# Residual before key variance, short power before the long one, and the choice of experts cut in two, in a two-layer adaLN kernel

## What is computed

```python
h = _layernorm(x) * (1 + ca) + sa
q = x @ w_q;  kv = x @ w_kv                  # 16 heads of 64, keys are values
q = q*cos + rot(q)*sin;  kv = kv*cos + rot(kv)*sin
lkv = _ln(concat([prev_window, window]), ln_local_g, ln_local_b)
pkv = softmax(gkv_seg @ w_proj)              # over the 16 tokens of a segment
gkv = _ln(einsum('bnsd,bnsr->bnrd', gkv_seg, pkv), ln_global_g, ln_global_b)
attn = softmax(masked(concat([q @ gkv.T, q @ lkv.T])))
x = x + ga * (attn @ concat([gkv, lkv]) @ w_out + b_out)
h = _layernorm(x) * (1 + cb) + sb            # input of the experts
topk_vals, topk_idx = top_k(h @ router_w, 2) # of 4 experts
```

## Time and profile before

| what | value |
|---|---|
| median of 3 runs | 1746.96 us (1745.7 to 1750.88) |
| the profiled execution | 1739.43 us |
| its span in the trace | 1737.6 us |
| PE, DVE, ACT, POOL busy over the span | 78%, 64%, 54%, 47% |
| layer-0 attention, slots 0 to 8 (97 to 661 us): PE, DVE, ACT, POOL busy | 441.9, 413.5, 341.0, 283.1 of 564 us |
| mean granted clock of TensorE there | 0.88 |

### The profile page before, as it was taken

How to read it: one execution, slowest core, us unless ns; L and a number is a source line. 1 busy time by engine, 2 the same in 40 slices (tenths; PEclk the granted TensorE clock), 3 DMA queues, 4 the chain that set the end, 5 groups by cost and what they waited for, 6 DMA issues and landing times. The chain is left out here.

```text
span 1737.6 us, 31729 instructions
## 1 busy us (share of the span) xinstructions
PE 1351.8 (78%) x8970; PEld 1077.2 (62%) x8970; DVE 1112.3 (64%) x2581; ACT 939.1 (54%) x2747; POOL 812.6 (47%) x824
## 2 busy tenths in 40 slices
PE   2267786697877984897998998994899988999552
PEld 0044564464645764897998897992566666676452
DVE  4575787877978544648447547442578888888522
ACT  1155564565756763666666666662556555555110
POOL 2446646555475312564665564663344544432103
PEclk7588898888988986999999999996889899989576
DMA  6300000000000005020020000006111111220063
GB/s 211 106 2 3 1 9 3 7 9 0 8 2 7 9 7 205 20 109 10 10 103 15 11 12 8 13 9 193 35 22 31 26 24 34 33 31 10 12 194 112
DMA packets 127182, 72.28 MB, mean 42 GB/s; under 512 B 78296, under 2 KB 118488, under 8 KB 126680
## 3 DMA queue, kind: packets, MB, share of 16 engines
q1 hardware_dynamic: 116664, 60.95, 12.3%
q0 software_dynamic: 3200, 6.56, 1.5%
q10 hardware_dynamic: 7200, 3.41, 0.7%
HBM read 53.26 MB, written 17.12 MB: 41 GB/s over the span
## 5 line engine op out<-in xcount | busy, mean ns | idle before, releaser
L1433 POOL TENSOR_TENSOR hl<-hid,hh 128x256 fp32r<-128x256 f32 x396 | 293.2, 742 | 221.2 <-ACT hh L1410 217.4
L1476 DVE SCALAR_TENSOR_TENSOR hid<-GU,gub,sg 128x256 f32<-128x256 f32 x396 | 190.3, 481 | 194.5 <-ACT sg L1404 111.8
L1304 PE MATMUL GU<-xh,wh 128*128 128x256 f32 x792 | 233.5, 295 | 39.4 <-DVE wl L1452 30.3
L1404 ACT ACTIVATE sg<-GU,gub 128x256 f32<-128x256 f32 x396 | 188.2, 475 | 123.6 <-PE GU L1306 122.1
L1305 PE MATMUL GU<-xl,wh 128*128 128x256 f32 x792 | 225.6, 285 | 0.0
L1306 PE MATMUL GU<-xh,wl 128*128 128x256 f32 x792 | 225.6, 285 | 0.0
L1840 ACT ACTIVATE prob<-S,negmax 128x256 f32<-128x256 f32 x256 | 119.2, 470 | 164.3 <-DVE negmax L2225 162.2
L1304 PEld LDWEIGHTS GU<-xh,wh 128*128 128x128 f32 x792 | 152.4, 192 | 48.9 <-issue 27.1
L1410 ACT CAST hh<-hid 128x256 fp32r<-128x256 f32 x396 | 158.1, 399 | 27.0 <-DVE hid L1476 25.8
L1716 PE MATMUL S<-kpad,qn 128*128 128x512 f32 x256 | 152.0, 679 | 1.5 <-POOL kpad L1960 1.4
L1305 PEld LDWEIGHTS GU<-xl,wh 128*128 128x128 f32 x792 | 152.8, 193 | 0.0
(11 more groups left out here) (289 smaller groups left out, 3263.9 us busy)
## 6 DMA issues: line engine op xcount, KB each, us to landing
raw<-in_expert_w SPq DMA_DIRECT2D x4, 2688.0 KB, 12.3
modb<-mod_d SPq DMA_DIRECT2D x2, 2688.0 KB, 15.0
list<-zero SPq DMA_DIRECT2D x5, 1024.0 KB, 9.7
raw<-in_expert_w SPq DMA_DIRECT2D x4, 1152.0 KB, 6.6
wa<-in_w SPq DMA_DIRECT2D x16, 256.0 KB, 3.5
wb<-in_w SPq DMA_DIRECT2D x16, 256.0 KB, 4.3
kpad<-rel_d SPq DMA_DIRECT2D x1, 3072.0 KB, 13.3
qkv_d<-qkvT SPq DMA_DIRECT2D x24, 128.0 KB, 4.5
```

The source lines that it names most:

```text
L1304: pe.matmul(out, lhs[0], rhs[0], start=start, stop=False, skip_group_check=True)
L1404: act.activation(sg[:, c % BUFS], GU[c % BUFS][:, 0:TT], ACT.Silu, bias=gub[:, GATE, e * CH0 + c:e * CH0 + c + 1]).then_inc(silu, 1)
L1433: pool.tensor_tensor(hl[:, b], hid[:, b], hh[:, b].bitcast(F32), ALU.subtract).then_inc(hid_lo, 1)
L1476: dve.scalar_tensor_tensor(out=hid[:, c % BUFS], in0=GU[c % BUFS][:, TT:2 * TT], scalar=gub[:, UP, e * CH0 + c:e * CH0 + c + 1], in1=sg[:, ...
```

## The change

On DVE, `residual` moves ahead of `kv_variance` in pair 2. On POOL, the power of the second layernorm moves ahead of `key_rstd`. `choose` is cut after the difference of the two logits: the one-hot rows and the counts become `count_choices`, which runs in pair 6, between the query rotation and `pooled_keys`. No instruction is added or taken away. Whole diff:

```diff
@@ -941,6 +941,10 @@
                 dve.wait_ge(t_step, T + 2)
                 dve.tensor_copy(topf[:], topi[:, :, 0:2]).then_inc(t_step, 1)
                 dve.tensor_tensor(ew[:, 0, :], top[:, :, 1], top[:, :, 0], ALU.subtract).then_inc(t_step, 1)
+
+            def count_choices(b):
+
+                T = T_STEPS * b
                 dve.wait_ge(t_step, T + 3)
                 for k in range(2):
                     i = dve.tensor_tensor(hot[:, k], cst("iota")[:, None, 0:E0].broadcast_to([P, TILES, E0]),
@@ -1008,9 +1012,10 @@
                         segment_softmax(slot, b)
                     if early and hp == 2:
                         segment_weights(b)
-                        kv_variance(b)
                     if late and hp == 2:
                         residual(slot, l)
+                    if early and hp == 2:
+                        kv_variance(b)
                     if early and hp == 3:
                         weights_back(slot, b)
                         if known_zero(b):
@@ -1032,6 +1037,8 @@
                     if late and hp == 5:
                         router_rows(slot, l)
                         choose(slot, l)
+                    if late and hp == 6:
+                        count_choices(l)
                     if early and hp == 6:
                         pooled_keys(slot, b, np_)
                     if norm and hp == 6:
@@ -1157,11 +1164,11 @@
                     if norm and hp == 0:
                         pool.wait_ge(ln_step, 6 * r + 3)
                         pool.tensor_tensor(rs[:], rs[:], half[:, 0:TILES], ALU.pow).then_inc(ln_rstd, 1)
-                    if early and hp == 2:
-                        key_rstd(b)
                     if late and hp == 2:
                         pool.wait_ge(r_step, R_STEPS * l + 5)
                         pool.tensor_tensor(rs2[:], rs2[:], half[:, 0:TILES], ALU.pow).then_inc(ln2_rstd, 1)
+                    if early and hp == 2:
+                        key_rstd(b)
                     if early and hp == 3:
                         normalise(b, np_)
                         if not known_zero(b):
```

## The result

The changed kernel takes 1736.79 us (median of 20 runs, 1723.2 to 1746.36), the kernel before 1745.62 us on the same chips (20 runs, 1733.58 to 1763.22). The ratio is 0.9936, 95% interval 0.9915 to 0.9957: 11.2 us less, faster by more than 0.3%, where 15.5 us less was forecast (1731.5; range 1716 to 1745). One of the seven executions of the kernel with the powers alone took 2380.55 us at a mean granted clock of 0.65, and is left out of its time and ratio.

What follows compares the result with a forecast made beforehand. Bound: PE's wait for `h` in layer-0 attention, DVE held by POOL's bulk multiplies. 26.5 us from G's earlier start, -15 clock, +4 divided choice: 15.5 us off 1746.96, giving 1731.5 us, range 1716 to 1745.

Steps and rivals of the forecast that it cites:

- What bounds the stretch: Layer-0 attention, pair 3: PE waits 69.3 us for `h`, whose DVE instructions POOL's bulk multiplies hold; the long power does not.
- rival E: POOL in pair 2: the long power holds DVE after all; 5 to 7 us lost a slot, 1783 us; chance 0.03.
- Parts 1 and 2: Pair 2: residual ahead of key variance on DVE, short power ahead of long on POOL; `h` 9 us earlier in slot 4.
- part 1: DVE, pair 2: residual ahead of the key variance; DVE stands 1.4 us for L515, cost to the path taken as 0.
- What is late next: PE at G (L432), pair 4: waits for POOL's `wk`, so G's start gains only 26.5 us over six slots.
- The clock: PE behind G: two idles bring the low clock, costing 2.5 us a slot, 15 us in all, bounds 0 and 23.
- A: PE's clock does not fall; all 26.5 us stay, but POOL may hold the moved piece; 1724 us; chance 0.12.
- D: PE's clock stays low through pair 5 and on, 6.7 us a slot; slower, 1756.5 us; chance 0.07.
- B: PE behind G: slot 0's low clock in every slot, 23 us lost; 1739.5 us; chance 0.15.
- Part 3: DVE, pairs 5 and 6: choice of experts divided, counts moved to pair 6; 4 us gained, bounds -7 and +4.
- rival C: Pair 6: POOL blocks the moved counts on DVE and key transposes come late; 1742.5 us; chance 0.08.

Runs made afterwards that it cites:

- the powers alone: Kernel before with only POOL's two powers exchanged in pair 2, the short one ahead of the long one: 1733.5 us, ratio 0.9912 to the kernel before.
- the order alone: Changed kernel with the counts of the chosen experts back in pair 5; only residual and short power moved: 1734.17 us, ratio 0.9955 to the kernel before.
- the long power first: Changed kernel with POOL's two powers back in their old order, residual still first on DVE: 1752.48 us, ratio 1.0009 to the kernel before.
- the split alone: Kernel before with only the counts of the chosen experts moved from pair 5 to pair 6: 1741.23 us, ratio 0.9989 to the kernel before.
- the idle matmuls: Changed kernel with unread matmuls in slots 1 to 6, eight before PE's wait for `h`, ten before `wk`: 1727.74 us, ratio 0.9888 to the kernel before.
- `wk` first: Changed kernel with POOL's `wk` products ahead of the two `V` multiplies in pair 3: 1732.12 us, ratio 0.9927 to the kernel before.

## Why the prediction was right, and where its sum was off

**What bounds the stretch: right.** Putting the long power back first restores the 72.5 us wait and the time of before. That POOL's multiplies hold DVE and its long power does not is seen in one slot of that run (0.43 us inside the power, 1.89 inside the multiplies). So rival E is dead, and with it the rule of the Trainium skill (SBUF — State Buffer, "Who interferes with whom") as far as this power goes; for the multiplies it holds. Kind and width were not tried apart: the power has 32 columns and the multiplies have 1024.

**Parts 1 and 2: right in each number to within 0.3 us, but part 1 is not needed.** The residual waited 1.48 us for L515 (forecast 1.4); the variance ended, at T, 5.6 us after L515 (5.4), L764 came 3.3 us behind that (3), `h` at T + 6.0 (5.7), free. What the prediction costed at nothing, the 1.0 to 1.4 us for the reciprocal, was indeed hidden: in slot 4 PE stood 1.20 us for ScalarE's `prob` and then still 2.88 us for `h`. But the later variance puts the long power, and with it `wk`, 0.9 us later than the exchange of the powers alone.

**What is late next: right, the wait a little shorter.** The new wait at L432 was forecast at 3 to 5 us in slots 1 to 5. It took 3.56, 2.72, 3.08, 1.76 and 3.27 us there, and 6.79 in slot 6. G started where the sum had it, since `wk` sets that: 13.5 us behind T in slot 4 (13.4). How much earlier G starts in a slot (its gain, less the gain already there at the scores of pair 3) was forecast as 3.4, 6.6, 4.5, 6.5, 4.5 and 0.9 us, 26.5 in all, and measured as 4.0, 6.5, 4.4, 6.4, 4.4 and 1.4, 27.0 in all.

**The clock: right mechanism, the term too small.** This is the term that was mis-sized. I took 2.5 us a slot, by half of slot 0's. From G to the scores of pair 5 slots 1 to 5 took 7.9, 8.2, 8.3, 7.8 and 8.5 us, against 5.1 to 5.3: with G's gain in each slot that is 2.7 to 3.2 us, 17.7 in all with slot 6. The low clock lasted 5.8 to 7.3 us behind G.

For what comes later the prediction had no term. From the scores of pair 7 of slot 4 to those of pair 3 of slot 5, where PE's code is the same, before and then after:
```profile
447.00:477.70 30.70, 25.81 (x191) 18.97 (x189) 27.68 (x54) 22.34 (x70) 11.63 (x8) 1.00 0.03 9
```
```profile
438.90:471.40 32.50, 30.32 (x190) 22.07 (x188) 26.27 (x54) 21.44 (x69) 9.36 (x7) 0.84 0.03 9
```
The mean clock of 0.84 means 10.4 us at 1.2 GHz, where before there were none, and the stretch is 1.8 us longer. From slot 2 to 3 it is the same, 2.0 us. From slot 1 to 2 it is 1.5 us, with 5.9 us at the low clock before and 10.2 after; from slot 3 to 4 it is 1.4 us, with 10.2 us in both, so there the length of the spell does not explain it; from slot 5 to 6 the stretch gained 2.5 us, with 10.2 before and 3.4 after. That is 4.2 us lost in all. It can't be put down to the change: in the profiles of other kernels these five stretches together differ as much. They take 158.7 us before and 162.9 after, 159.5 with the order alone, 159.1 with the long power first, and 167.7 with the split alone, where PE's wait for `h` is that of before. What sets off such a spell, far from the waits that the change made, is open.

Rivals A and D fell: the clock did fall, and it stayed low for less than D's 10.2 us behind G. B was half right: 2.7 to 3.2 us a slot lie between my 2.5 and its 3.9, and the time of 1736.8 is nearer to B's 1739.5 than to my 1731.5. What A added, that without the low clock POOL is late and holds the moved counts, is what the run with the idle matmuls showed.

**Part 3: right.** The moved piece took 0.9 us in slot 4 (436.44 to 437.35), not held: rival C fell. From the scores of pair 5 to those of pair 7 slots 1 to 5 gained 1.2, 0.1, 1.2, 0.7 and 1.2 us, 4.4 in all (forecast 4), though the clock moves these too. The trace with the split alone has 5.2, and that with the order alone 0.8; the times of those two runs can't confirm it. It holds only while POOL is done with its rotation: with the idle matmuls, and with `wk` first, the counts took up to 2.9 and 3.3 us.

**The sum.** In the two profiles 27.0 for G, -17.7 for the clock behind it, +4.4 for the split and -4.2 for the later stretches give 9.5 us; small differences in slots 0, 6 and 7 make it the 10.6 us by which the attention ended earlier. The timed difference, 11.2 us by the ratio and 8.8 by the medians, agrees. Of the forecast's three terms only the clock is off by more than 1 us, 2.7 us more lost; the 4.2 us of the later stretches stand in no term, and by the spread above they may be chance.

## What to carry to other kernels

When a wait of one engine hides another's, work out the next one before pricing the gain: here 69 us of waiting gave 27 us at the next step and 11 in time. Look for which instructions of a neighbour hold an engine (here its multiplies and adds over 128x1024) and which do not (here its power over 128x32), and put short instructions beside the latter; one exchange of two POOL instructions did that, and no gain of the reordering on DVE is seen. Removing a loss of clock wins little where another engine is late right behind it: 18 us won behind G were 16 us lost again in pairs 5 and 6. Once one engine works without a break, reordering only moves the wait from consumer to consumer, and taking one instruction off it is what pays.

## What the runs showed of the hardware

- A power on POOL over 128x32 takes 5.43 us and over 128x2 0.69 us, and DVE instructions with two SBUF inputs run beside it at their free 0.43 us. Beside POOL's multiplies over 128x1024 (1.9 us each) the same instructions take 1.9 us, beside its adds over 128x1024 (2.4 us each) 2.3 us, and a DVE add over 128x1024 beside them took 3.36. The one that comes first is not held: L913 took 0.43 us when it began 0.09 us ahead of a multiply, and 2.09 when it began 0.09 us behind one.
- Breaking one idle of PE of 7.7 to 12.7 us a slot into two of about 3 us raised the time at the low clock from 123 to 146 us, and the time in which PE works at it from 73 to 127. Matmuls that nobody reads in these idles cut the low clock to 72 us; in time that brought some 8 us.
- From the scores of pair 7 to those of pair 3 of the next slot, slots 2 to 3 and 4 to 5 took 30.7 us with no low clock and 32.5 to 32.6 with 10.2 us of it: 1.8 to 2.0 us for a spell.
